# P times V of a causal attention in three rounded passes, with the exponentials one step later

## The reference

```python
x = x + _layernorm(_L1_attn_ref(_layernorm(x, axis=-1), Wq, Wk, Wv, Wo), axis=-1)
# 4096 rows in the order of x as 2 batches of 2048; 2 query heads share one key and one value head of 128
q = rope(xn @ Wq[h].T); k = rope(xn @ Wk.T); v = xn @ Wv.T
p = softmax(causal(q @ k.T / sqrt(128)))
out = concat_h(p @ v) @ Wo.T
```

## Time and profile before

| what | value |
|---|---|
| median of 3 runs | 2033.57 us (2028.32 to 2036.43) |
| the profiled execution | 2031.22 us, its span 2029.4 us |
| mean granted clock of TensorE | 0.933 of full speed |
| TensorE matmuls, weight loads | 1728.3 us, 1311.6 us busy |
| VectorE, ScalarE, GpSimd | 1460.4, 979.5, 1022.9 us busy |
| causal attention, batch 0: load, row tiles | 1353.8 to 1394.7, 1394.7 to 1563.5 us |
| causal attention, batch 1: load, row tiles | 1569.5 to 1615.4, 1615.4 to 1800.9 us |

### The profile page before, as it was taken

The page is one execution under the profiler, slowest core; times in us unless marked ns, Lnnn a source line. Parts: engine busy times, 40 slices in busy tenths (PEclk is TensorE's granted clock), DMA queues, the critical chain, the costliest instruction groups (busy, mean ns, idle before and its releaser), DMA issues. The chain is left out here.

```text
span 2029.4 us, 36910 instructions
## 1 busy us (share of the span) xinstructions
PE 1728.3 (85%) x13596; PEld 1311.6 (65%) x13596; DVE 1460.4 (72%) x3403; ACT 979.5 (48%) x2163; POOL 1022.9 (50%) x680
## 2 busy tenths in 40 slices
PE   3899999998489999999998599947898689969993
PEld 2677877787355665666655476625786577758782
DVE  5688778877578877787884678878776777864234
ACT  2455565655325665665654354423332254326664
POOL 3466656555317887787774166642000400356654
PEclk9899999999759999999998799968999899979996
DMA  5112112211100000000000133349200000016763
GB/s 171 74 69 85 64 72 77 79 64 69 44 0 1 2 1 1 1 1 1 2 1 1 40 102 94 100 117 233 49 1 1 1 1 1 21 56 205 208 221 113
DMA packets 78467, 124.08 MB, mean 61 GB/s; under 512 B 11824, under 2 KB 43440, under 8 KB 77776
## 3 DMA queue, kind: packets, MB, share of 16 engines
q1 hardware_dynamic: 73744, 112.31, 18.2%
q0 software_dynamic: 4544, 9.41, 1.4%
HBM read 59.19 MB, written 28.94 MB: 43 GB/s over the span
## 5 line engine op out<-in xcount | busy, mean ns | idle before, releaser
L1088 ACT ACTIVATE mb_pt<-mb_stb 128x1024 f32<-128x1024 f32 x256 | 250.6, 1021 | 129.7 <-PE mb_stb L1233 128.5
L938 DVE TENSOR_REDUCE mb_mxp<-mb_p1b 128x1 f32<-128x512 f32 x352 | 231.2, 684 | 46.0 <-PE mb_p1b L1217 42.0
L1138 POOL TENSOR_TENSOR mb_psum<-mb_pt 128x1024 f32<-128x1024 f32 x70 | 166.8, 2386 | 131.0 <-ACT mb_pt L1088 130.7
L351 DVE TENSOR_TENSOR ma_tr<-ma_pbank,ma_cs 128x512 f32<-128x512 f32 x256 | 161.9, 682 | 67.9 <-PE ma_pbank L66 55.0
L1143 POOL TENSOR_TENSOR mb_psum<-mb_psum,mb_pt 128x1024 f32<-128x1024 f32 x84 | 200.6, 2388 | 20.0 <-ACT mb_pt L1088 9.8
L441 POOL TENSOR_TENSOR ma_qt<-ma_tr,ma_swp 128x512 f32<-128x512 f32 x64 | 82.3, 1288 | 158.0 <-DMA ma_swp<-ma_tr 157.9
L2544 PE MATMUL mc_pv<-mc_pt,mc_v 128*128 128x256 f32 x544 | 146.6, 394 | 17.2 <-DVE mc_pt L2347 17.0
L1217 PE MATMUL mb_p1b<-mb_ks,mb_qs 96*128 96x512 f32 x352 | 146.8, 458 | 5.3 <-DVE mb_mxp L938 1.6
L1834 POOL TENSOR_TENSOR mc_frs<-mc_fve,mc_half 128x4 f32<-128x4 f32 x8 | 8.1, 1013 | 272.6 <-DVE mc_fve L1818 272.6
L490 ACT ACTIVATE ma_e<-ma_sbank,ma_mx 128x80 f32<-128x80 f32 x512 | 119.6, 367 | 49.7 <-DVE ma_mx L358 49.7
L1233 PE MATMUL mb_stb<-mb_qs,mb_ks 98*128 98x512 f32 x512 | 143.1, 401 | 0.4 <-ACT mb_pt L1088 0.4
(11 more groups left out here) (423 smaller groups left out, 4756.2 us busy)
## 6 DMA issues: line engine op xcount, KB each, us to landing
ma_swp<-ma_tr SPq DMA_DIRECT2D x256, 128.0 KB, 2.0
md_wslot<-d_weights SPq DMA_DIRECT2D x39, 516.0 KB
d_xs<-mw_blank SPq DMA_DIRECT2D x1, 16899.0 KB, 76.2
mb_gb<-b_gates SPq DMA_DIRECT2D x64, 256.0 KB, 3.3
md_xs<-d_xs SPq DMA_DIRECT2D x39, 131.0 KB, 3.3
md_work<-d_ret SPq DMA_DIRECT2D x8, 512.0 KB, 5.4
mg_X<-x SPq DMA_DIRECT2D x4, 512.0 KB, 9.8
ma_cs<-cs SPq DMA_DIRECT2D x1, 2048.0 KB, 9.8
```

The costliest lines, as they stand in the source:

```text
L351: nc.vector.tensor_tensor(tr[:, G % TRS, part, :, :], pbank[:, i % 2, :].rearrange("p (c t) -> p c t", c=2), cs[:, b // 2, part, None, :]. ...
L938: nc.vector.tensor_reduce(mxp[:, r // NCH, r % NCH:r % NCH + 1], pass_bank(r), AXX, ALU.max).then_inc(p1_max, 1)
L1088: nc.scalar.activation(pt[:, T % RING, :, :].rearrange("p (b h) q -> p b (h q)", b=2), stb[:, 2 * (i % 2):2 * (i % 2) + 2, :], ACT.Exp, sc ...
L1138: nc.gpsimd.tensor_tensor(total, pt[:, T % RING, :, :], pt[:, (T + 1) % RING, :, :], ALU.add).then_inc(summed, 1)
```

## The change

In the row tiles, P times V becomes three fp32r passes. ScalarE rounds the turned P from `tb` into `pth`, VectorE then subtracts it from `tb` into `ptl`, and the product of a pair waits for `ptl`. V is kept as `vh` and `vl`, the second made by VectorE in the load (`v_lows`). On ScalarE the exponentials of `ahead(r, s-1)` now stand behind the rounding of step s; those of the last step stand at the end of the row tile. In the load the normalisation goes from VectorE to ScalarE (scale `S.r`, bias `nbias`, which VectorE makes in the block before).

```diff
                     stats_vector(nc, dve, X, S, 1e-5, weights)
+                    for half in range(2):
+                        tiles = slice(half * BT, (half + 1) * BT)
+                        dve.wait_ge(S.powed, 2 * half + 2)
+                        nc.vector.scalar_tensor_tensor(nbias[:, tiles], S.mean[:, tiles, 0], -1.0, S.r[:, tiles], ALU.mult,
+                                                       ALU.mult).then_inc(shifted, 1)
...
-        v = m.sb("v", [P, KT, D])
+        vh = m.sb("vh", [P, KT, D], F32R)
+        vl = m.sb("vl", [P, KT, D], F32R)
...
-        pt = m.sb("pt", [P, 2, BLK])
+        pth = m.sb("pth", [P, 2, BLK], F32R)
+        ptl = m.sb("ptl", [P, 2, BLK], F32R)
...
 VectorE
+                def v_lows(b, i):
+                    dve.wait_ge(v_copied, b * BB + i + 1)
+                    at = slice(i * BPT, (i + 1) * BPT)
+                    nc.vector.tensor_tensor(vl[:, at, :], vbank(i).rearrange("p (a b) -> p a b", b=D),
+                                            vh[:, at, :].bitcast(F32), ALU.subtract).then_inc(v_low, 1)
                 def load(b):
-                    norm(b, 0)
-                    norm(b, 1)
                     low(b, 0)
                     for i in range(BB):
                         rope(b, R * i)
                         if i > 0:
                             rope_low(b, R * i - 1)
-                        if i + 2 < BB:
-                            norm(b, i + 2)
                         rope(b, R * i + 1)
                         rope_low(b, R * i)
                         if i + 1 < BB:
                             low(b, i + 1)
+                        v_lows(b, i)
...
-                            if not by_act(K):
-                                dve.wait_ge(pt_mm, b * NP + K + 1)
-                                if K >= 2:
-                                    dve.wait_ge(pv_mm, b * NP + K - 1)
-                                wd = pair_of(r, s) * HC * P
-                                nc.vector.tensor_copy(pt[:, K % 2, 0:wd], tb[:, K % 2, 0:wd]).then_inc(pt_copied, 1)
+                            dve.wait_ge(pt_high, b * NP + K + 1)
+                            wd = pair_of(r, s) * HC * P
+                            nc.vector.tensor_tensor(ptl[:, K % 2, 0:wd], tb[:, K % 2, 0:wd], pth[:, K % 2, 0:wd].bitcast(F32),
+                                                    ALU.subtract).then_inc(pt_low, 1)
 ScalarE
+                def norm(b, i):
+                    n = b * BB + i
+                    act.wait_ge(shifted, b + 1)
+                    if i >= 2:
+                        act.wait_ge(xt_mm, n - 1)
+                    for s in range(BPT):
+                        tile = n * BPT + s
+                        nc.scalar.activation(xn[:, i % 2, s, :], X[:, tile, :], ACT.Identity, bias=nbias[:, tile:tile + 1],
+                                             scale=S.r[:, tile:tile + 1]).then_inc(xn_ready, 1)
                 def load(b):
+                    norm(b, 0)
+                    norm(b, 1)
                     copies(b, 0)
                     copies(b, 1)
                     for i in range(BB):
                         act.wait_ge(v_mm, b * BB + i + 1)
-                        nc.scalar.activation(v[:, i * BPT:(i + 1) * BPT, :], vbank(i).rearrange("p (a b) -> p a b", b=D),
+                        nc.scalar.activation(vh[:, i * BPT:(i + 1) * BPT, :], vbank(i).rearrange("p (a b) -> p a b", b=D),
                                              ACT.Copy).then_inc(v_copied, 1)
+                        if i + 2 < BB:
+                            norm(b, i + 2)
...
                         for s in range(pairs[r]):
                             K = firstp[r] + s
-                            exps(b, r + 1, ahead(r, s))
+                            act.wait_ge(pt_mm, b * NP + K + 1)
+                            if K >= 2:
+                                act.wait_ge(pv_mm, b * NP + K - 1)
+                            wd = pair_of(r, s) * HC * P
+                            nc.scalar.activation(pth[:, K % 2, 0:wd], tb[:, K % 2, 0:wd], ACT.Copy).then_inc(pt_high, 1)
+                            if s > 0:
+                                exps(b, r + 1, ahead(r, s - 1))
+                        exps(b, r + 1, ahead(r, pairs[r] - 1))
 TensorE
-                            pe.wait_ge(v_copied, b * BB + i - 1)
+                            pe.wait_ge(v_low, b * BB + i - 1)
...
-                    pe.wait_ge(v_copied, (b + 1) * BB)
+                    pe.wait_ge(v_low, (b + 1) * BB)
...
-                        dve_done, act_done = copied_before(K - 1)
-                        pe.wait_ge(pt_copied, b * copied_before(NP)[0] + dve_done)
+                        pe.wait_ge(pt_low, b * NP + K - 1)
...
-                        last = nc.tensor.matmul(pv[:, 0:HC * P], v[:, t, :], pt[:, K % 2, a * HC * P:(a + 1) * HC * P],
-                                                start=(t == 0), stop=(t == r))
+                        at = slice(a * HC * P, (a + 1) * HC * P)
+                        last = matmul_split(nc, pv[:, 0:HC * P], vh[:, t, :], vl[:, t, :], pth[:, K % 2, at], ptl[:, K % 2, at],
+                                            start=(t == 0), stop=(t == r))
```

More of the change, by code:

```diff
@@ L2041, in causal_attention @@
         rp = room[:, at[4]:at[5]].rearrange("p (i c) -> p i c", c=BLK)
+        nbias = m.sb("nbias", [P, TILES])
+        shifted = m.sem("shifted")
         with Mem(nc, "c0_") as t:
@@ L2111, in causal_attention @@
         v_copied = m.sem("v_copied")
+        v_low = m.sem("v_low")
         proj_mm = m.sem("proj_mm")
@@ L2121, in causal_attention @@
         pt_mm = m.sem("pt_mm")
-        pt_copied = m.sem("pt_copied")
-        pt_shared = m.sem("pt_shared")
+        pt_high = m.sem("pt_high")
+        pt_low = m.sem("pt_low")
         pv_mm = m.sem("pv_mm")
@@ L2137, in causal_attention @@
         NP = firstp[KT]
-        SHARED = False
         R = 1 + HC
@@ L2154, in ahead @@
             return todo[s * quota:(s + 1) * quota]
[L2156 to L2161, removed]
         def vbank(i):
@@ L2230, in between @@
                         LF.variances(nc, dve, 3)
[L2232 to L2239, removed]
                 def low(b, i):
@@ L2455, in _ @@
                             K = firstp[r] + s
-                            if by_act(K):
-                                act.wait_ge(pt_mm, b * NP + K + 1)
-                                if K >= 2:
-                                    act.wait_ge(pv_mm, b * NP + K - 1)
-                                wd = pair_of(r, s) * HC * P
-                                nc.scalar.activation(pt[:, K % 2, 0:wd], tb[:, K % 2, 0:wd], ACT.Copy).then_inc(pt_shared, 1)
-                            exps(b, r + 1, ahead(r, s))
+                            act.wait_ge(pt_mm, b * NP + K + 1)
[6 more added lines that the diff above has]
+                        exps(b, r + 1, ahead(r, pairs[r] - 1))
                         if b == BACK:
@@ L2521, in transposes @@
                     if K >= 2:
-                        dve_done, act_done = copied_before(K - 1)
-                        pe.wait_ge(pt_copied, b * copied_before(NP)[0] + dve_done)
-                        if by_act(K - 2):
-                            pe.wait_ge(pt_shared, b * copied_before(NP)[1] + act_done)
+                        pe.wait_ge(pt_low, b * NP + K - 1)
                     for a in range(pair_of(r, s)):
@@ L2534, in values @@
                     K = firstp[r] + s
-                    dve_done, act_done = copied_before(K + 1)
-                    if by_act(K):
-                        pe.wait_ge(pt_shared, b * copied_before(NP)[1] + act_done)
-                    else:
-                        pe.wait_ge(pt_copied, b * copied_before(NP)[0] + dve_done)
+                    pe.wait_ge(pt_low, b * NP + K + 1)
                     if s == 0 and r > 0:
```

## The result

The kernel after takes 2095.11 us (median of 4 runs, 2093.41 to 2096.88), the kernel before in the same sitting 2032.19 us (4 runs, 2028.32 to 2036.43). The ratio is 1.0317, with a 95% interval of 1.0296 to 1.0338. The change makes the kernel 3.2% slower, 63 us. The forecast was 2086 us in a range of 2052 to 2110.

The account below looks back on a forecast made before the run. The prediction took the row tiles to be bound by TensorE and the load by VectorE. It summed 2031.2 + 49 (row tiles) + 3 (next layer's rows) - 5 (load) + 8 (clock) = 2086.2 us, range 2052 to 2110.

Parts of the forecast that it names:

- 49 + 3 + 8 = 60 us: Over both batches: 49 us for the row tiles, 3 for batch 1's next-layer rows, 8 for TensorE's lower clock.
- the hand calculation: Row tile 14 of batch 0 followed step by step on the earlier trace's clock: 3.0 us longer, TensorE idling 2.35 us.
- The row tiles: Causal attention: 24.5 us more a batch, 49 in two, product saving included; row tiles 8 to 14 cost 2.7 each.
- The clock: Row tiles 8 to 14: idle TensorE falls to 1.2 GHz; half of 14 at 1.2 us, 8 us, bounds 0 and 28.
- Rival 3: The clock falls in every row tile with a held rounding, also the small ones: 2110 us; chance 0.09.
- held roundings: Row tiles 8 to 14: roundings stand behind exponentials waiting for head 1's bias; called the larger term; chance as drawn 0.76.
- the longer way: Transposes, ScalarE's rounding, VectorE's subtraction, product: 2.03 us, so 1.38 us a pair instead of 1.30 even with free engines.
- TensorE's saving of 20.4 us: P times V in three fp32r passes, 0.72 us a pair: 272 key tiles x 0.075 us, if TensorE stays the bound.
- the estimate of 30 us: P times V: by the skill's four fp32 passes, three of equal length save a quarter of 0.435 us each.
- Rival 1: TensorE stays the bound: products save 20.4 us and the load 5, giving 2006 us; chance 0.08.
- The load: Norms on ScalarE, V's remainders on VectorE: about 0 in batch 0, -5 us in batch 1.
- Batch 1's rows for the next layer: After row tiles 5 and 6, ScalarE's 8 writes delay output copy and next rounding: 1.4 to 2.2 us, twice, 3 us.

Follow-up runs that it names:

- the run that kept TensorE busy: The kernel after with 16 added matmuls of 128 bf16 columns ahead of the held product of row tiles 7 to 14; 2083.71 us, ratio 1.0252.
- spread: The kernel after with only ScalarE's order altered: head 1's exponentials start one step later still, dealt out over the remaining steps; 2060.75 us, ratio 1.0148.
- no wait for the bias: The kernel after with a constant bias of zero, each exponential waiting only for its own chunk's maximum; 2044.07 us, ratio 1.0059.
- rounded once by VectorE: The kernel after with one VectorE rounding of P, no subtraction, exponentials in their own step, third pass reusing the rounded P; 2026.55 us, ratio 0.9974.

## Why the prediction came true, and where it didn't

The mechanism that was put down is in the trace step by step, and the sum was 9 us low (2086.2 against 2094.68 of the profiled execution). These 9 us are 2.8 in the two loads and 5.7 outside the stage, where nothing was edited. For row tiles 1 to 15 the sum had 49 + 3 + 8 = 60 us, and 60.0 were measured. That it fits so well is luck: row tiles 8 to 14 cost 51.5 us and not 46 (38 and the clock's 8), and everything else in these terms 8.5 us and not 14 (1 of the 14 was for row tile 0, which is measured with the load). By the prediction's own steps, in row tile 14 (times from its first transposes, 1533.98 in the hand calculation, 1561.05 in the kernel after):

| step | predicted | measured |
|---|---|---|
| scores of head 1 that need a bank | 6.39 | 6.23 |
| head 1's bias done (before: 11.70) | 12.42 | 12.03 |
| rounding 4 starts | 13.80 | 13.41 |
| product 4 starts | 15.19 | 14.78 |
| idle time ahead of it | 2.35 | 1.93 |
| length of the row tile | 19.46 | 20.07 |

**The row tiles.** Row tiles 8 to 14 were to cost 19 us a batch; they cost 22.9 and 28.5. Part of that is the clock, a term of its own in the sum. The price without it was about right: row tile 13 of batch 0 has a held product and no fall of the clock behind it, and is 2.5 us longer, against 2.7 predicted. Row tile 7 cost 1.4 and 0.7 us against 1.7, row tiles 3 to 6 together 0.3 and 2.5 against 1.6, and row tile 15 0.85 and 0.66 against 0.7.

**The clock** was mis-sized: 8 us predicted, about 12 or more measured. The granted clock lost 20 us more than before (35.4 - 15.7), and the run that kept TensorE busy shows 11.8 us of time for 17.1 of them. I had counted 1.2 us in half of 14 row tiles. In the trace each fall loses 1.7 us of clock or twice that, and 11 of the 14 have one, five of them in batch 0. The idle time alone does not say where: the held product of row tile 13 waits as long as that of row tile 14, and the clock stays up behind it:

```profile
1557.40 0.39 PE L64 MATMUL mc_pv<-mc_pth,mc_vh 128*128 128x256 f32 x1 [1.95 <-DVE mc_ptl L2340]
```

```profile
1557.00:1560.00 3.00, 2.30 (x16) 1.96 (x16) 1.55 (x3) 1.94 (x6) 0.00 (x0) 1.00 0.00 0
```

The Trainium skill's page "TensorE: Matmul & The Clock Gate", section "HAM oscillation — how this bites in real kernels", tells of bursts that fall to the lower clock at every wait, of some 3 to 5 us each. The traces agree only in part: the waits of 1.81 to 2.15 us in row tiles 8 to 14 of batch 0 have a fall in five cases of seven. Rival 3, more falls in the small row tiles too and 2110 us, did not happen: row tiles 1 to 7 of both batches together lose 7.6 us of clock against 8.9 before.

**The weight between held roundings and the longer way** is what the prediction left unproven. It called holding the larger term. Row tiles 8 to 14 of batch 0 against before, in us (the 22.9 hold 8.5 us of lost clock, the others none):

| | roundings held | not held |
|---|---|---|
| with the subtraction | 22.9 | 7.8 (spread), 1.8 (no wait for the bias) |
| without it | 4.0 | -3.7 (rounded once by VectorE) |

Taking away either one takes away most of the 22.9 us, so neither is the cause alone. Which is the larger depends on the run that stands for "not held". By the spread order, holding costs 7.7 us without the subtraction and 15.1 with it, the subtraction 11.5 without holding and 18.9 with it. By the run without the wait for the bias, holding costs 21.1 us with the subtraction, and the subtraction 5.5 without holding. The last cell also has the copy on another engine. So the order of the two is not shown. The subtraction acts three times: it stands between rounding and product (0.69 us); it stands ahead of the maxima, so that head 1's bias comes 0.8 us later than without it (it starts at 11.9 us in the row tile against 11.1); and the two together make an idle time of 1.93 us out of one of 0.77, behind which the clock falls in this row tile. The hand calculation had the first two, the bias too late by 0.4 us, but never worked out what the row tile would be without each. Over the whole kernel taking the subtraction away gives 81 us, taking away the wait for the bias 52, and spreading the exponentials 34.

**TensorE's saving of 20.4 us** was wrong. The step that failed is "an fp32r pass takes 0.12 us, a pair 0.72": after transposes a pair takes 0.80 to 0.82. With 0.05 to 0.07 us saved for most of the 144 pairs, some 10 us or less were to be had, an estimate. The Trainium skill's four passes for true fp32 (page "FP8 and Floating Point Precision", section "TensorE Precision Notes") would be 0.48 us at 0.12 each, an estimate; 0.435 was measured, no run shows the number of passes, and the estimate of 30 us made from that rule was further off still. None of the kernels run with all three passes and the subtraction beats the kernel before. Rival 1 (2006 us) was out of reach for this reason too, apart from the waits.

**The load.** Predicted about 0 and -5; measured +1.1 and -3.3. In batch 1 the norm alone gives 5.1 us, where the prediction's terms without the remainders of V make 7.7 (5, and 2.7 for the remainders). The remainders cost 1.8 us of these 2.7 (56.04 us against 54.26 with the norm alone). **Batch 1's rows for the next layer**, 3 us in row tiles 5 and 6, were not seen: these are 0.2 and -0.1 us against before. The clock loses 1.7 us less in them than before, so at most some 2 us can be hidden there.

**What was not looked for.** The copy on VectorE was itself held in the kernel before, 3.53 us in row tile 5. The chance to gain lay there: ScalarE's copy with spread exponentials is 1.2% faster than before (0.9855 to 0.9900), with the fp32 product left alone. Row tiles 11 to 13 of batch 0 of that kernel are still 0.3 to 0.9 us longer than before, while row tile 14 is not. In them the last products still wait for ScalarE's copies, 0.34, 0.39 and 0.58 us in all; in row tile 14 none does.

## What to carry to other kernels

A copy put on a queue that also holds work waiting for a reduction is late by that wait, so the order in that queue is worth more than the engine's share of busy time; but cost each way of being late alone and together: here holding alone cost 4.0 us, the subtraction alone 7.8 and the two together 22.9, in part because TensorE's clock then fell in most of these row tiles. Price a cheaper matmul form where it will stand, next to the instructions that precede it there, and not inside a run of its own kind. And look in the kernel before for the same copy being held by other work: moving it may be the gain, without the new arithmetic.

## What the runs showed of the hardware

- The first fp32r pass of 256 columns behind fp32 transposes takes 0.20 to 0.22 us from start to start, the next ones 0.12. Behind other fp32r passes the first takes 0.12 too:

```profile
1568.55 0.40 PE L66 MATMUL mc_sb<-mc_kql,mc_kqh 128*128 128x512 f32 x1
1568.78 0.28 PE L64 MATMUL mc_pv<-mc_pth,mc_vh 128*128 128x256 f32 x1
1568.90 0.28 PE L65 MATMUL mc_pv<-mc_pth,mc_vl 128*128 128x256 f32 x1
```

- Behind 1.93 us of idle time (row tile 14) the granted clock went to 0.50, and the fall lost 1.7 us of clock; behind 0.77 and 1.02 us it stayed at 1.00 there, the latter with sixteen small matmuls in the gap. The length of the one wait does not decide it. Row tile 11 of batch 0 has its wait of 1.81 us in the kernel after and with the norm put back, and the clock falls in it only in the first. In the run with ScalarE's copies and exponentials in their own step, seven waits of 1.46 to 1.77 us in row tiles 8 to 14 of batch 0 have no fall. And in batch 1 of the kernel without the subtraction the clock is at 0.50 behind a wait of 1.00 us:

```profile
1696.00 0.69 PE L64 MATMUL mc_sb<-mc_kqh 128*128 128x512 f32 x1 [1.00 <-ACT mw_room L2439]
```

```profile
1696.20:1699.20 3.00, 3.00 (x9) 2.09 (x9) 2.72 (x18) 1.57 (x5) 0.00 (x0) 0.50 0.00 0
```

- In the two sittings in which the kernel before took 2082 and 2084 us, row tile 13 of batch 1 is 27 to 30 us longer in all kernels traced (the kernel before was not traced then), the stretch after the last output copy 20 to 25 us, and engines stand still in that row tile for a reason that the trace names only "remote". These are VectorE's waits in the kernel with ScalarE's copies in row tiles 4 to 7, 26 us together; what held it is not settled:

```profile
1763.37 0.69 DVE L2341 COPY mc_pt<-mc_tb 128x512 f32<-128x512 f32 x1 [7.56 <-remote]
1771.11 0.69 DVE L2341 COPY mc_pt<-mc_tb 128x512 f32<-128x512 f32 x1 [7.06 <-remote]
1783.03 0.69 DVE L2341 COPY mc_pt<-mc_tb 128x512 f32<-128x512 f32 x1 [11.22 <-remote]
```
